# A selective-scan layer on one core: which states the product with C reads, what it waits for, and held expert pairs on two banks

## The reference, cut to what matters

```
h = exp(clip(dt*A, -10, 0)) * h + dt * B * x        # per channel and state
hn = norm of h over the 16 states
h = h * min(1, 10 / hn)   only where t % 16 == 15     # the bound
y[t] = sum over n of C[t, n] * h[n]  + D * x[t]
```

## Time and profile before

| what | value |
|---|---|
| median of 3 runs | 4447.61 us (4446.76 to 4454.78) |
| the profiled execution | 4455.33 us |
| its span | 4453.3 us |
| granted PE clock, mean | 0.964 |

### The profile page before, as it was taken

How to read it: one execution, slowest core, us unless ns; L and a number is a source line. 1 busy time by engine, 2 the same in 40 slices (tenths; PEclk the granted TensorE clock), 3 DMA queues, 4 the chain that set the end, 5 groups by cost and what they waited for, 6 DMA issues and landing times.

```text
span 4453.3 us, 72570 instructions
## 1 busy us (share of the span) xinstructions
PE 3967.3 (89%) x18752; PEld 2605.9 (59%) x18752; DVE 3625.9 (81%) x9566; ACT 3121.9 (70%) x9232; POOL 2589.8 (58%) x1284
## 2 busy tenths in 40 slices
PE   6788888888888888888888888868999999999999
PEld 5666666666666666666666666634455454454454
DVE  4899999999999999999999999864657666666677
ACT  6899999999999999999999999834333333333321
POOL 4898989889888888898988988840000000000000
PEclk8899999999999999999999999989999999999999
DMA  3111111111111111111111111110000000000000
GB/s 112 53 54 55 54 59 50 59 54 58 54 58 54 58 54 54 54 53 60 50 60 53 58 54 58 53 37 22 7 16 7 16 16 6 16 16 6 7 8 10
DMA packets 91556, 187.43 MB, mean 42 GB/s; under 512 B 16160, under 2 KB 58016, under 8 KB 90912
## 3 DMA queue, kind: packets, MB, share of 16 engines
q1 hardware_dynamic: 91424, 185.92, 13.0%
HBM read 168.05 MB, written 17.83 MB: 42 GB/s over the span
## 4 chain that ended last, share of the span: by engine, by line
PE 39%; issue 22%; POOL 18%; DVE 17%; ACT 3%; DVEq 1%; POOLq 1%; SPq 0%; DMA 0%; ACTq 0%
PE ps L734 21%; POOL prod L356 11%; PE ps L839 5%; DVE macc L1071 4%; POOL hb L364 3%; PE ps L874 3%; PE ps L856 2%; POOL xcv L380 2%; ACT zr L417 2%; DVE sg L1254 2%; POOL u L373 1%; PE ps L833 1%; PE ps L789 1%; PE ps_dA L874 1%; DVE xin L1185 1%
## 5 line engine op out<-in xcount | busy, mean ns | idle before, releaser
L734 PE MATMUL ps<-w_x,mxT 128*128 128x512 f32 x4096 | 1962.3, 607 | 114.6 <-DVE macc L1071 114.6
L1071 DVE SCALAR_TENSOR_TENSOR macc<-ps,gate,macc 128x256 f32<-128x256 f32 x2048 | 978.7, 478 | 492.6 <-PE ps L734 408.8
L980 DVE TENSOR_TENSOR_SCAN hb<-ps_dA,hb 128x1088 f32<-128x1088 f32 x512 | 1240.5, 2423 | 90.1 <-POOL hb L364 77.7
L356 POOL TENSOR_TENSOR prod<-hb,cbc 128x1024 f32<-128x1024 f32 x512 | 1122.5, 2192 | 234.3 <-DVE hb L999 234.0
L364 POOL TENSOR_TENSOR hb<-u,bbc 128x1024 f32<-128x1024 f32 x512 | 1203.1, 2350 | 75.1 <-POOL prod L356 70.9
L417 ACT ACTIVATE zr<-dt,aneg 128x128 f32<-128x128 f32 x4096 | 1239.8, 387 | 0.0
L734 PEld LDWEIGHTS ps<-w_x,mxT 128*128 128x128 f32 x4096 | 736.0, 194 | 819.6 <-issue 601.4
L700 PE MATMUL ps<-ident,prod 128*128 128x128 f32 x4096 | 554.6, 295 | 12.8 <-POOL prod L356 9.6
L700 PEld LDWEIGHTS ps<-ident,prod 128*128 128x128 f32 x4096 | 513.0, 153 | 25.3 <-POOL prod L356 22.5
L426 ACT ACTIVATE ps_dA<-zr 128x1024 f32<-128x1024 f32 x512 | 518.2, 1012 | 0.0
L477 ACT ACTIVATE ex<-lgt,ms 128x16 f32<-128x16 f32 x128 | 39.1, 305 | 357.9 <-DVE ms L1019 357.9
(11 more groups left out here) (197 smaller groups left out, 5102.8 us busy)
## 6 DMA issues: line engine op xcount, KB each, us to landing
bbc<-bcd SPq DMA_DIRECT2D x128, 512.0 KB, 3.7
cbc<-bcd SPq DMA_DIRECT2D x128, 512.0 KB, 3.8
xt<-in_x SPq DMA_DIRECT2D x128, 128.0 KB, 3.7
x2d<-macc SPq DMA_DIRECT2D x64, 128.0 KB, 1.7
out_dram<-macc SPq DMA_DIRECT2D x64, 128.0 KB, 1.7
w_x<-in_w_x SPq DMA_DIRECT2D x1, 4096.0 KB, 14.8
hb<-x2d SPq DMA_DIRECT2D x32, 128.0 KB, 2.3
sz<-x2d SPq DMA_DIRECT2D x16, 128.0 KB, 2.2
```

The lines of the kernel that those rows point to most:

```text
L356: TT(dst, states, cc, ALU.mult).then_inc(M["prodp"], 1)
L734: last = mm(banks[p % len(banks)][:], mxT[k][:, j, :], w_x[:, j, p * 512:(p + 1) * 512], start=(j == 0), stop=(j == KD - 1))
L980: V.tensor_tensor_scan(states, dA, states, 0.0, ALU.mult, ALU.add).then_inc(M["scan"], 1)
L1071: STT(macc[k][:], banks[(e // 2) % len(banks)][:, (e % 2) * D:(e % 2 + 1) * D], gate[k][:, e:e + 1], macc[k][:], ALU.mult, ALU.add).then_i ...
```

## The change

The product no longer takes columns 1 to 16 of a chunk but columns 0 to 15: the bounded last state of the chunk before stands in column 0, so nothing of the chunk's own bound is needed, and the product waits for `scan` alone. It covers the steps shifted by one, so that at even chunks the first column belongs to the quarter before and is a multiply of its own. The last step of a tile (column 16 of chunk 7) comes in `last_product`, which waits for `hs`. The in-place bound of the last column (L999) is left at chunk 7 only. `inputs(c + 2)` now stands in slot c, and waits also for the squares and the bound of chunk c, which read the last column that it overwrites. `bound` waits for the product before, which reads column 0 of the buffer that it writes. The quarter sums wait for products 2, 4, 6 and 7 in place of 1, 3, 5 and 7, and the load of `cbc[0]` for product 4 in place of 3. The held pairs use `G` = `(G0, G1)`.

```diff
+        QUARTER_ENDS = (2, 4, 6, 7)
+        def states_product(c, s0, s1):
+            t0 = c * CH + s0 - 1
+            half, at, w = t0 // HT, t0 % HT, s1 - s0
+            return (prod[t0 // QT % 2][:]...[:, :, :, t0 % QT:t0 % QT + w],
+                    hb[c % 2][:]...[:, :, :, s0:s1],
+                    cbc[half][:, :, at:at + w]....broadcast_to([P, EB, N, w]))
...
-                    products_done(sp, i, HC - 1)
+                    products_done(sp, i, HC)
                     sp.dma_start(cbc[0][:], spread_rows(1 - k, 1, 0)).then_inc(M["cc0"], 16)
...
             def product(i, k, c):
-                g.wait_ge(M["hs"], AHEAD + i * NC + c + 1)
-                g.wait_ge(M["cc0" if c < HC else "cc1"], AHEAD + (i + 1) * 16)
+                g.wait_ge(M["scan"], AHEAD + i * NC + c + 1)
                 g.wait_ge(M["y"], AHEAD + i * 4 + c // QC - 1)
-                dst, states, cc = chunk_product(c)
-                TT(dst, states, cc, ALU.mult).then_inc(M["prodp"], 1)
+                if c == 0:
+                    g.wait_ge(M["cc0"], AHEAD + (i + 1) * 16)
+                    multiply(c, 1, CH).then_inc(M["prodp"], 1)
+                elif c % QC == 0:
+                    multiply(c, 0, 1)
+                    if c == HC:
+                        g.wait_ge(M["cc1"], AHEAD + (i + 1) * 16)
+                    multiply(c, 1, CH).then_inc(M["prodp"], 1)
+                elif c < NC - 1:
+                    multiply(c, 0, CH).then_inc(M["prodp"], 1)
+                else:
+                    multiply(c, 0, CH)
+            def last_product(i):
+                g.wait_ge(M["hs"], AHEAD + i + 1)
+                multiply(NC - 1, CH, SL).then_inc(M["prodp"], 1)
             def inputs(i, k, c):
...
                 products_done(g, i if c >= 2 else i - 1, (c - 2) % NC)
+                g.wait_ge(M["sq"], AHEAD + i * NC + c - 1)
+                g.wait_ge(M["st0"], AHEAD + i * NC + c - 1)
...
             def step(i, k, stages):
                 for c in range(NC):
-                    if c == 0 and "B" in stages:
-                        product(i - 1, 1 - k, NC - 1)
-                    if c > 0 and "S" in stages:
-                        product(i, k, c - 1)
-                    if c < NC - 1 and "S" in stages:
-                        inputs(i, k, c + 1)
+                    if "S" in stages:
+                        product(i, k, c)
                     extra(i, k, c, stages)
-                if "G" in stages:
-                    inputs(i + 1, 1 - k, 0)
+                    if c == NC - 1 and "S" in stages:
+                        last_product(i)
+                    if c < NC - 2 and "S" in stages:
+                        inputs(i, k, c + 2)
+                    if c >= NC - 2 and "G" in stages:
+                        inputs(i + 1, 1 - k, c + 2 - NC)
...
             def norms(i, c):
-                a.wait_ge(M["hs"], AHEAD + q)
+                a.wait_ge(M["st0"], AHEAD + q)
+                if c == 0:
+                    a.wait_ge(M["hs"], AHEAD + i)
...
             def sum_states(i, h):
-                products_done(pe, i, (h + 1) * QC - 1)
+                products_done(pe, i, QUARTER_ENDS[h])
...
                 if b == 0 and t * (X // 2) + p in LATE:
                     m, q = late_pair(t * (X // 2) + p)
-                    experts_mm(m, m % 2, q, q + 1, GM)
+                    if t * (X // 2) + p == LATE[0]:
+                        pe.wait_ge(R["ac"], AHEAD + m * (X + 1) + 2 * q + 1)
+                        pe.wait_ge(M["yt"], AHEAD + NTILES * 2)
+                    experts_mm(m, m % 2, q, q + 1, G)
...
             def bound(i, c, top=1.0):
                 v.wait_ge(M["ne"], AHEAD + q + 1)
+                products_done(v, i, c - 1)
                 STT(nxt[:, :, 0:1]..., factor, top, last, ALU.min, ALU.mult).then_inc(M["st0"], 1)
-                STT(last, factor, 1.0, last, ALU.min, ALU.mult).then_inc(M["hs"], 1)
+                if c == NC - 1:
+                    STT(last, factor, 1.0, last, ALU.min, ALU.mult).then_inc(M["hs"], 1)
...
-                    expert_sums(m, m % 2, 2 * q, 2 * q + 2, GM)
+                    expert_sums(m, m % 2, 2 * q, 2 * q + 2, G)
```

More of the change, by code:

```diff
@@ L252, in flat @@
             return t[:].rearrange("p a b -> p (a b)")
[L254 to L259, removed]
+        QUARTER_ENDS = (2, 4, 6, 7)
+        def states_product(c, s0, s1):
+            t0 = c * CH + s0 - 1
+            half, at, w = t0 // HT, t0 % HT, s1 - s0
+            return (prod[t0 // QT % 2][:].rearrange("p n e t -> p e n t")[:, :, :, t0 % QT:t0 % QT + w],
+                    hb[c % 2][:].rearrange("p (e n) s -> p e n s", e=EB)[:, :, :, s0:s1],
+                    cbc[half][:, :, at:at + w].rearrange("p (e n) s -> p e n s", e=1).broadcast_to([P, EB, N, w]))
         block = ctx.enter_context(nc.Block())
@@ L348, in _, with multiply @@
             TT = nc.gpsimd.tensor_tensor
+            def multiply(c, s0, s1):
+                dst, states, cc = states_product(c, s0, s1)
+                return TT(dst, states, cc, ALU.mult)
             def product(i, k, c):
-                g.wait_ge(M["hs"], AHEAD + i * NC + c + 1)
-                g.wait_ge(M["cc0" if c < HC else "cc1"], AHEAD + (i + 1) * 16)
+                g.wait_ge(M["scan"], AHEAD + i * NC + c + 1)
                 g.wait_ge(M["y"], AHEAD + i * 4 + c // QC - 1)
-                dst, states, cc = chunk_product(c)
-                TT(dst, states, cc, ALU.mult).then_inc(M["prodp"], 1)
+                if c == 0:
[13 more added lines that the diff above has]
+                multiply(NC - 1, CH, SL).then_inc(M["prodp"], 1)
             def inputs(i, k, c):
@@ L934, in slot @@
                     m, q = late_pair(t * (X // 2) + p)
-                    experts_mm(m, m % 2, q, q + 1, GM)
+                    if t * (X // 2) + p == LATE[0]:
+                        pe.wait_ge(R["ac"], AHEAD + m * (X + 1) + 2 * q + 1)
+                        pe.wait_ge(M["yt"], AHEAD + NTILES * 2)
+                    experts_mm(m, m % 2, q, q + 1, G)
                 if b > 0:
-                    experts_mm(n + NTILES, n % 2, p, p + 1, G4 if b == NB else G, fresh=(b in (1, NB) and t == 0))
+                    experts_mm(n + NTILES, n % 2, p, p + 1, G4 if b == NB else G, fresh=(b == NB and t == 0))
                 m = routed(b, t)
```

## The result

The changed kernel takes 4585.5 us, median of 4 runs (4582.7 to 4590.9), against 4447.2 (4440.5 to 4454.8): ratio 1.0312, interval [1.0293, 1.0331]. It is 138 us slower where 49 us faster was forecast. The profiled span is 4584.2 against 4453.3.

A forecast was written before the change was run, and what follows sets the result against it. No engine was full: four queues hand one tile round, the chain running over DVE. Steady tiles -33, first and last tiles -10, held pairs -6 gave -49, so 4398 us from 4447.6, range 4358 to 4436.

The forecast's parts named there:

- the four rivals: Full gain, 4364 (0.22); POOL and lock eat it, 4435 (0.17); slower by L1144, 4470 (0.11); POOL waits equally long, 4440 (0.05).
- Scan 3's wait: Chunk 3's scan no longer waits for POOL's inputs: gain 0.46 in three tiles of four, 0.34 us per tile.
- Scans 6 and 7: Chunk 6's 0.33 is lost, its wait moving to L997 behind ACT; chunk 7's scan gains 0.50 us per tile.
- Chunk 7: After scan 7, L1061 is held by POOL's x1b or last product: 0 to 0.7 lost, 0.35 us taken.
- Chunk 3: L1190 starts 4.68 after scan 3, product 3 ends at 4.8, so POOL holds it for nothing: no loss.
- POOL's load: POOL's multiplies become 960 elements (2.05 us) and 64 elements (0.33, bounds 0.2 to 0.74): net 0.8 us more per tile.
- L1144: After scan 0, L1144 waits out POOL's product 0 and ends 0.14 us later, hidden behind the PE wait at L1163.
- rival 3: Product 0 starts just ahead of L1144 and holds it: 0.35 to 0.7 us more per tile, 4470 us; chance 0.11.
- L999 gone: Dropping this DVE operation at seven chunks gains 0 to 0.09 us each at chunks 2 to 5: 0.10 per tile.
- First and last tiles: Fewer POOL waits and a shorter last product in the first and last tiles: -10 us (0 to -16).
- Held pairs: In sequence 0, PE's waits for DVE before seven pairs shrink: -6.4 us (-3 to -9).
- Rival 2: Small multiplies near 0.7, xcv 0.4 late, L1061 held 0.65: steady tiles gain 0, 4435 us; chance 0.17.

The follow-up runs named there:

- the memsets: Changed kernel with 120 idle DVE instructions at its start and four DVE operations (L1144, L1190, L1193, L1061 before) turned into memsets: 4397.8 us, ratio 0.9889.
- the control: Kernel before with the same four DVE operations (L1144, L1190, L1193, L1061) turned into memsets that read nothing: 4396.1 us, ratio 0.9883.
- before_held: Kernel before with only the twelve held pairs put on two banks: 4441.7 us, ratio 0.9986.
- after_pad120: Changed kernel with 120 more semaphore increments at the start of DVE's program, nothing else different: 4475.1 us, ratio 1.0062.
- before_dve6: Kernel before with DVE alone leaving two tiles more unrolled ahead of its loop, same work and order: 4572.1 us, ratio 1.0278.

## Why the prediction was wrong

**The step that failed** is one that the prediction never took. "The change part by part" prices operations, waits and locks, and holds the loop's jump back to cost what it costs now. The change adds four instructions of DVE ahead of the loop and two inside it. The old loop ended at most one instruction short of an edge, and the new one lies across it: 121.6 us in the 56 tiles, where the prediction had nothing. None of the four rivals had it, so all the chance given to "slower" stood on another mechanism. A program's size had no row in the prediction, though the instruction queue's line was on the page, with 80 packets, none of them between 500 and 2500 us.

Without the stall the sum would have been wrong too. 2553.64 less 2531.70 is +22, or +0.39 per tile, where -0.59 was forecast, and that with the clock's help: L789, which the prediction left where it was, is slow in fewer tiles, and among the tiles without it the difference is +0.46. Term by term (a wait of scan 3 lies in the time of chunk 2, one of scan 7 in that of chunk 6):

- *Scan 3's wait, forecast -0.34.* Chunk 2 falls by 0.41, from 6.17 to 5.76; among the tiles without a slow L789 by 0.26. In this term the mechanism was right.
- *Scans 6 and 7, forecast -0.50 together (the first wait handed on to the bound, the second gained); chunks 5 and 6 measured -0.07 and -0.25.* Both waits for POOL are gone (0.32 and 0.48 on average before), and the bound of chunk 6 waits 0.29 for ACT in place of 0.05, as forecast. Not forecast: at chunk 5 too the reduction of ACT's squares starts later, 3.60 behind its scan in place of 3.36.
- *Chunk 7, forecast +0.35 for the lock alone; measured +0.93.* The lock at L1061 adds 0.42 (0.63 - 0.21). The rest has no term: I followed ACT only to chunk 6. ACT works 14 units without a pause behind it, the squares of chunk 7 come later against the scan (ACT, kernel after, same tile as above):

```profile
1373.55 4.19 ACT L441 ACTIVATE zr<-dt,aneg 128x128 f32<-128x128 f32 x14
1377.65 0.30 ACT L456 ACTIVATE sq<-hb 128x64 f32<-128x64 f32 x1
```

  and L1017 starts 3.75 behind its scan (1377.98 - 1374.23), with 0.30 of waiting, where L988 started 3.31 behind before. That takes back 0.44 of what the scans before had gained. From the start of scan 4 to this reduction the chain takes 20.0 before and 20.1 after, on average: it looks as if ACT sets it, which no run tests.
- *Chunk 3, forecast nothing; measured +0.35.* "L1190: nothing" failed. POOL is later than I reckoned: product 3 ends 5.47 after the scan (1592.13 - 1586.66, the scan's start in the same timeline), not 4.8, and L1223 goes from 0.48 to 0.83 on average. With the memsets the changed kernel gains 0.35 more here than the control, which puts it down to the lock.
- *POOL's load.* The groups of 500 to 2500 us in the kernel after:

```profile
L356 POOL TENSOR_TENSOR prod<-hb,cbc 128x1024 f32<-128x1024 f32 x167 | 375.4, 2248 | 7.5
L356 POOL TENSOR_TENSOR prod<-hb,cbc 128x960 f32<-128x960 f32 x168 | 353.8, 2106 | 63.1 <-DVE hb L1009 63.1
L356 POOL TENSOR_TENSOR prod<-hb,cbc 128x64 f32<-128x64 f32 x168 | 71.6, 426 | 50.8 <-DVE hb L1030 42.7 <-DVE hb L1009 8.1
```

  0.43 for the small multiply against 0.33, within the bounds; 2.11 against 2.05, 2.25 against 2.17; and a gap of 0.29 to 0.31 between product and inputs, 0.17 before. POOL's busy time grows by 1.3 us per tile in place of 0.8. It is busy 41.8 of 45.6 us, 92%, where over 93% was said.
- *L1144, forecast 0.14 and hidden:* 0.28 longer on average (0.59 to 0.87). Chunk 0 grows by 0.29 and chunk 1 falls by 0.43, so it is hidden, as said. The tile of 1575.18 is a milder case of what rival 3 described: product 0 had started 1.26 ahead of L1144 and held it for 0.6, and it did not decide.
- *L999 gone, forecast -0.10:* no gain of its own is seen; chunk 4 stays 4.98. Where L999 stood, the scan of chunks 1 to 6 now waits 0.13 behind the bound.
- *First and last tiles, forecast -10; measured about 0.* Against before_held, after_pad120 differs by +0.5 from the first scan to the 56 tiles, by +0.9 from them to the last scan, and by -0.9 behind it; the changed kernel by +0.7, +1.4 and -3.5.
- *Held pairs:* -6.4 forecast; 5.9 measured alone by the medians, 8.7 in the traces. Right.

Rival 2 (POOL and the lock eat the gain) was the nearest to the steady tile, at 0 against +0.39.

What stays open: how much of the 0.44 at chunk 7 comes from ACT, since no run changes its work, and why the pause differs. It is 5.07, 4.87 and 4.37 us on average with 2, 4 and 8 idle instructions ahead of the old loop, 3.85 in before_dve6 and 3.47 in the changed kernel.

## What to carry to other kernels

Ahead of any change to an engine's loop or to its prologue, find where that loop's first and last instruction lie in its program; a change of a few instructions can cost more than all that it reorders, and moving the loop by idle instructions is a cheap control for it: two of them gave the old kernel the stall, and 120, for 8 to 10 us, took it from the new one. When one scan stops waiting, follow each engine of the chain to the end of the tile: a wait that moves one step down (ACT's row to the squares) has not gone. An operation of GpSimd moved in time is also a lock moved in time, for each VectorE operation that it comes to lie beside.

## What the runs showed of the hardware that was not expected

- A loop of 372 instructions on VectorE costs 5.3 us more per jump when moved by two: 4447.6 against 4589.4 us. With the other moves and in the changed kernel it is 4.5 to 5.1.
- The profile puts this stall down to an unrelated semaphore (POOL hb, 94.0 us of L1009); the packets of the instruction queue, 80 against 217, and a consumer whose inputs ended long ago are what give it away.
- A one-input VectorE operation from SBUF to SBUF stands still beside GpSimd as well: 0.65 us for 16 elements a partition. A memset in its place takes 0.07 beside the same, and the next one-input operation (L1096) is held in its stead, 0.49 in place of 0.23.
- GpSimd's multiply of 64 elements a partition takes 0.43 us.
- With the pause at the jump L815 takes 317 ns a matmul on average and 285 without it; the mean granted clock of the 56 tiles is 0.94 and 0.97. This is 25 of the stall's 121.6 us.
